# One sweep of a warp-and-blend kernel: the subtraction of the old feature on TensorE in every row, and a gate product over all 128 array rows

## The reference

```python
center = einsum('nchw,oc->nohw', feature, w_center)
step = relu(einsum('nchw,oc->nohw', feature, w_step))
prob = sigmoid(einsum('nchw,oc->nohw', feature, w_prob))
offset = center * step
th = minimum(round(gh + offset[0]), h - 1); tw = minimum(round(gw + offset[1]), w - 1)
tgt = mod(th * w + tw, h * w)
sample = grid.at[tgt].set(grid)            # a scatter: the last writer of a target wins
sampled = grid_sample_bilinear(feature, sample)
proped = sampled * prob + feature * (1 - prob)
return feature * prob + proped * (1 - prob)
```

## Time and profile before

| | us |
|---|---|
| median of 3 runs | 8082.5 (8072.88 to 8084.91) |
| the profiled execution, its own time | 8102.3 |
| its span | 8100.6 |
| TensorE busy | 5697.9 |
| VectorE busy | 5391.9 |
| GpSimd busy | 4030.2 |
| ScalarE busy | 3005.0 |
| mean granted clock of TensorE | 0.78 |

### The profile page before, as it was taken

One profiled execution on the slowest core, in us unless ns is written; L12 is line 12 of the kernel. 1 busy time (PEld: TensorE's weight loads), 2 busy tenths in 40 slices (PEclk: granted clock), 3 DMA queues, 4 the chain that ended last, 5 costly groups with the idle time before them and its releaser, 6 DMA issues. The chain is left out here.

```text
span 8100.6 us, 91641 instructions
## 1 busy us (share of the span) xinstructions
PE 5697.9 (70%) x26004; PEld 2956.5 (36%) x26004; DVE 5391.9 (67%) x12584; ACT 3005.0 (37%) x5830; POOL 4030.2 (50%) x8123
## 2 busy tenths in 40 slices
PE   5653645466756886689767676799677656878888
PEld 3432323233423443355443332354333222333333
DVE  6447774385754544866789735777889735777777
ACT  3432223122212332222112225666336545454545
POOL 6657453374434353634225336644335355666664
PEclk8876766688866886789877777899887777676777
DMA  7985569567556786666426776755235645666666
GB/s 278 354 306 194 175 210 276 170 235 240 187 163 204 282 291 217 223 206 211 155 91 233 223 261 212 216 160 167 91 112 173 166 143 177 209 214 214 213 215 193
DMA packets 543221, 1672.95 MB, mean 207 GB/s; under 512 B 125182, under 2 KB 180339, under 8 KB 501012
## 3 DMA queue, kind: packets, MB, share of 16 engines
q1 hardware_dynamic: 223708, 827.34, 33.3%
q10 hardware_dynamic: 254552, 763.42, 25.1%
q0 software_dynamic: 64480, 76.57, 5.1%
HBM read 949.39 MB, written 727.71 MB: 207 GB/s over the span
## 5 line engine op out<-in xcount | busy, mean ns | idle before, releaser
L1107 DVE TENSOR_TENSOR ps<-ps,arena 128x400 f32<-128x400 f32 x1600 | 929.1, 581 | 1853.5 <-PE ps L1286 657.3
L1416 ACT ACTIVATE arena<-ps 128x400 f32<-128x400 f32 x1600 | 800.8, 501 | 3155.7 <-PE ps L1270 1103.6
L1049 POOL TENSOR_TENSOR arena<-arena 128x32 f32<-128x32 f32 (+8 forms) x3013 | 941.9, 356 | 1910.6 <-PE ps L1312 1910.3
L1278 PE MATMUL ps<-arena,minus 128*128 128x400 f32 x2800 | 1625.5, 669 | 84.6 <-DVE arena L1109 84.2
L1326 PE MATMUL ps<-ident,arena 128*128 128x128 f32 x5000 | 916.5, 332 | 800.8 <-ACT arena L1390 469.3
L1295 PE MATMUL ps<-arena 128*64 128x400 f32 x3200 | 900.2, 646 | 602.4 <-ACT arena L1430 420.7
L1248 POOL DMA_INDIRECT arena<-table,gidx x800 | 871.5, 1089 | 843.7 <-PE ps L1295 552.8
L1390 ACT ACTIVATE arena<-ps 128x512 f32<-128x512 f32 (+1 forms) x1400 | 735.4, 551 | 1254.4 <-PE ps L1326 700.2
L1286 PEld LDWEIGHTS ps<-ident,arena 100*128 100x128 f32 x6400 | 833.5, 164 | 779.1 <-issue 642.3
L1326 PEld LDWEIGHTS ps<-ident,arena 128*128 128x128 f32 x5000 | 745.6, 204 | 988.4 <-ACT arena L1390 554.3
L1248 POOL DMA_INDIRECT arena<-table,arena x800 | 794.0, 992 | 528.8 <-issue 233.9
(11 more groups left out here) (212 smaller groups left out, 6216.8 us busy)
## 6 DMA issues: line engine op xcount, KB each, us to landing
arena<-x SPq DMA_DIRECT2D x200, 1600.0 KB
arena<-table SPq DMA_DIRECT2D x400, 800.0 KB
table<-arena ACTq DMA_DIRECT2D x400, 512.0 KB
y<-arena ACTq DMA_DIRECT2D x200, 800.0 KB
arena<-y SPq DMA_DIRECT2D x100, 1600.0 KB
out<-arena ACTq DMA_DIRECT2D x200, 800.0 KB
table<-arena ACTq DMA_DIRECT2D x200, 576.0 KB
conv<-arena ACTq DMA_DIRECT2D x800, 31.2 KB
```

The costliest lines, as they stand in the source:

```text
L1049: last = E.tensor_tensor(tmp[:, :, at:at + size], cols[:, :, y + to:end + to:step], cols[:, :, y:end:step], ALU.subtract)
L1107: V.tensor_tensor(d, d, g, ALU.mult).then_inc(s_mix, 1)
L1278: nc.tensor.matmul(ps[:, sums(r), 0:W], minus[:, :], tile(t)[:, r * W:(r + 1) * W], start=True, stop=False)
L1416: nc.scalar.activation(gate[r % 2], ps[:, 6 + r % GB, 0:W], ACT.Copy).then_inc(s_gcopy, 1)
```

## The change

In the last sweep the subtraction of the old feature is made by TensorE in every row: `lifted` and VectorE's L1104, with the semaphore between it and the multiplication, go. In all sweeps the gate product reads all 128 partitions of the gates' buffers (`gates_all`) and of `halves`, which grows from 24 to 128 partitions. What is not gate or weight in them is set to zero once: for two of the buffers and `halves` by VectorE at the start, for the third by GpSimd at the start of the fifth sweep, with a wait of SyncE before the first load into it. The loads write the same 24 partitions as before.

```diff
-        halves = sb("halves", [QUAD + 6 * HALF, HALF * 128], BF16)[QUAD:, :]
+        halves = sb("halves", [128, HALF * 128], BF16)
...
+        gates_all = [again(a, W, 128, BF16) for a in gates_at]
...
-                sp.wait_ge(s_init, 1)
+                sp.wait_ge(s_init, 2)
...
+                nc.vector.memset(halves[:, :], 0.0).then_inc(s_init, 1)
+                for a in range(2):
+                    nc.vector.memset(gates_all[a], 0.0)
...
-                nc.vector.tensor_copy(halves, halves32)
+                dve.wait_ge(s_init, 2)
+                nc.vector.tensor_copy(halves[QUAD:QUAD + 6 * HALF, :], halves32)
...
-            def lifted(r):
-
-
-                return listed and u_idx is None and r % 2 == 1
...
-                        if lifted(r):
-                            V.tensor_tensor(d, d, y, ALU.subtract).then_inc(s_less, 1)
-                            less[0] += 1
-                            dve.wait_ge(s_less, less[0])
                         V.tensor_tensor(d, d, g, ALU.mult).then_inc(s_mix, 1)
...
+                            if listed and j == RR - 1 and u_idx is not None:
+                                sp.wait_ge(s_blank, 1)
+                                alone(sp, "sp")
...
+                    if listed and u_idx is not None:
+                        nc.gpsimd.memset(gates_all[2], 0.0).then_inc(s_blank, 1)
...
-                        nc.tensor.matmul(ps[:, 6 + r % GB, 0:W], halves[:, m % HALF * 128:(m % HALF + 1) * 128], gates_in[j % RR],
+                        nc.tensor.matmul(ps[:, 6 + r % GB, 0:W], halves[:, m % HALF * 128:(m % HALF + 1) * 128], gates_all[j % RR],
                                          start=True, stop=True).then_inc(s_gate, 1)
...
-                        if not lifted(r):
-                            nc.tensor.matmul(ps[:, sums(r), 0:W], minus[:, :], tile(t)[:, r * W:(r + 1) * W], start=True, stop=False)
+                        nc.tensor.matmul(ps[:, sums(r), 0:W], minus[:, :], tile(t)[:, r * W:(r + 1) * W], start=True, stop=False)
...
-                                                    ident[0:STRIP, 0:STRIP], is_transpose=True, start=lifted(r) and q == 0, stop=not listed and q == STRIPS - 1)
+                                                    ident[0:STRIP, 0:STRIP], is_transpose=True, start=False, stop=not listed and q == STRIPS - 1)
```

More of the change, by code:

```diff
@@ L367, in _ @@
                     nc.vector.memset(w_conv[l][:, 10:], 0.0)
-                nc.vector.tensor_copy(halves, halves32)
+                dve.wait_ge(s_init, 2)
+                nc.vector.tensor_copy(halves[QUAD:QUAD + 6 * HALF, :], halves32)
                 nc.vector.tensor_copy(ident16[:, :], ident[:, :])
                 nc.vector.tensor_scalar(minus[:, :], ident[:, :], -1.0, None, ALU.mult).then_inc(s_init, 1)
-                dve.wait_ge(s_init, 2)
+                dve.wait_ge(s_init, 3)
         s_maps = sem("s_maps")
@@ L385, in build @@
         s_gatest = sem("s_gatest")
+        s_blank = sem("s_blank")
         s_path = sem("s_path")
@@ L390, in build @@
         tabled, rowed = [0], [0]
-        s_less, less = sem("s_less"), [0]
         s_fld = [sem(f"s_f_ld{a}") for a in range(4)]
```

## The result

The kernel takes 7890.06 us (median of 5 runs, 7851.52 to 7893.64) against 8072.88 us for the kernel before on the same chip (5 runs, 8067.68 to 8084.91): a ratio of 0.975, 95% interval 0.9719 to 0.9781. The profiled execution has a span of 7849.9 us; it is the fastest of its five, 39 us under their median, while the profiled execution before lies 29 us above this median of 8072.88.

The account below looks back on a forecast made before the run. TensorE was taken as the bound, often at half clock after waiting on ScalarE: 171 us off the last sweep plus 40 off the others takes 8102 to 7891, forecast as 7875 us since the profiled execution is 20 above the median; range 7760 to 8060.

Parts of the forecast that it names:

- The border of the gate product: TensorE, each row: each border of the 24-row product costs about 0.09 us; padding saves 36 us in the last sweep.
- The other sweeps: Mixing sweeps before the last: 30 us from 210 TensorE-bound rows plus 10 for the clock, 40 us less; bounds 0 and 150.
- The clock of the last sweep: TensorE, last sweep: share at half clock falls from 56% to 25%, so the granted clock rises from 0.72 to 0.87.
- The pause on ScalarE's L1430: TensorE's wait every four rows, last sweep: 3.5 us path fits in 3.6 us of rows, so most of 180.0 us goes.
- GpSimd's floor: Last sweep: two gathers a row, each 0.99 us plus 0.29 of issue, allow no less than 2.56 us a row.
- The landings: Last sweep: waits on landings of transfers, 7.4% of the chain, 97 us or 0.24 a row, do not go.
- transfers become the bound: Rival, last sweep: landings replace the pauses, 3.1 us a row, 70 us saved plus 20 elsewhere, about 7990 us; chance 0.18.
- gate product counts everywhere: Rival: clock rises in all four mixing sweeps, 150 us instead of 40, last sweep 2.65 us a row, 7680 us; chance 0.10.
- The exposed weight load: Rival: a 0.25 us load stands bare behind each gate product, last sweep only 31 us less, 8050 us; chance 0.03.
- The clock does not rise: Rival, last sweep: clock stays at 0.72, a row takes 3.6 us, kernel 130 us slower, 8210 us; chance 0.13.
- nothing: Rival: longer TensorE rows and fewer pauses cancel, 8080 us; chance 0.06.
- The clears: Clears on VectorE at the start and GpSimd before the fifth sweep: hidden, cost nothing; those on VectorE under 2 us if uncovered.

Follow-up runs that it names:

- 64-row: Kernel after the change, with the gate product over array rows 0 to 63 instead of 128: 8047.91 us, ratio 0.9904 to the kernel before.
- 72-row kernel: Kernel after the change, with the gate product over array rows 0 to 71 instead of 128: 7945.42 us, ratio 0.9763 to the kernel before.
- the move alone: Kernel after the change, but gate product on 24 rows again; only the last sweep's subtractions moved to TensorE: 8102.69 us, ratio 0.9958 to the kernel before.
- groups of eight: Kernel after the change, with GpSimd gathering in groups of eight rows instead of four in the last sweep: 8144.05 us, ratio 1.0024 to the kernel before.

## Why the prediction was right, and where its steps were not

The time was forecast at 7875 us in a range of 7760 to 8060, and is 7890. The total is right by luck: two steps miss in opposite directions.

**The border of the gate product** was priced at 0.09 us, and twice that where the product in front is a full one too. This term was mis-sized. The start of the subtraction after the gate product moved by 0.09 us, as forecast; but the subtraction is two products with a weight load each, and with the first load under the gate product what separates them shrinks as well, 0.11 us from its start to the transposes' (the earlier trace rows against the timeline after). A row in the two last sweeps thus saves 0.20 us; where a product over the full width of the array stands in front of the gate product, as transposes do in the two sweeps before, one more border of 0.09 us goes. The border in front of it after the 64-column one-hot products stayed, as forecast. The 64-row and 72-row kernels show that all of the row's saving is one step of shape.

**The other sweeps** were given 40 us, with 150 as the bound, because only 210 rows were taken to have TensorE as the limit. This step failed. 183 us are gone there in the profiled executions; over the ten profiles with at least 72 rows that share the code of these sweeps, the three windows sum to 5096 to 5168 us (mean 5137), against 5279 before and 5306 and 5261 with 24 and 64 rows, so the gain is 111 to 183 us. TensorE's saving of 149 us in the first of them became 65 us of time: only a part of it, but far more than 210 rows at 0.18 us could give. The last sentence of the prediction took a move of more than 100 us as a sign that "the gate product's width did more than its borders"; it came, and it came for the most part through the borders, not through the clock.

**The clock of the last sweep** was forecast at 0.87 and is 0.89. It does rise with the move alone (0.72 to 0.85). But the mix of products does not set it by itself, as the prediction's main choice had it: with the same mix it is 1.00 without the gathers and 0.81 with groups of eight. What it was to bring did not come: the move alone is worth 14 us. The last sweep gave 74 us of the 171 forecast, or 35 in the 72-row kernel.

**The pause on ScalarE's L1430** was to close, and most of its 180.0 us to go. This step failed: it is 197.1 us. The forecast row was 2.55 us of TensorE and 0.30 of waits, 2.85; the measured one is 2.11 / 0.89 = 2.37 and 0.74, 3.11. The comparison of 3.5 against 3.6 us was sound, as the run without gathers shows, but it started the 3.5 us at the recorded end of the one-hot products, and with gathers under way the multiplications of rows 3, 4, 7 and 0 start about 2 us later than that (medians of 1.8 to 2.1 us from row 40 on; before they were 1.1 to 1.5, with 0.6 for the subtraction in rows 3 and 7). It is mostly the counts of rows 3 and 7 that are late: there everything else that the multiplication waits for has long ended (by 1.9 and 1.3 us in the median), while in rows 4 and 0 it starts 0.1 us after the copy of the gate. GpSimd's floor, 2.56 us a row, was also short of what is behind it: after eight gathers of 1.25 us GpSimd waits 2.0 us (median) for a late count, so four rows cost 12.2 us, 3.05 each. That the count is held until GpSimd has finished is not shown. The forecast that GpSimd would be near 70% busy fails with it: 64%.

**The landings** were to stay at 7.4% of the chain, 97 us or 0.24 a row of the sum. The share stayed (7.4%), but the step is wrong: what stands there are releases that the profile cannot name, in front of VectorE's multiplication (102.5 us), ScalarE's copy of the gate and GpSimd's gathers (62.1 us), which wait for counts of other engines. They grow when bytes are taken out and are gone without the gathers. So this term of the sum is a part of the late counts and no price of transfers. The rival *transfers become the bound* named the last sweep's row (3.1 us) by the wrong mechanism: 30% fewer bytes change nothing, and only without gathers do landings of the table's rows become the wait. The rival *gate product counts everywhere* had the other sweeps' 150 us right, but not the clock as the main cause. *The exposed weight load* had it the wrong way round: the first load starts with the padded gate product, and it is behind the 24-row product that it had to wait. The Trainium skill, "TensorE: Matmul & The Clock Gate", The mechanism (in its Part 3), has a load overlap products in flight only where the row groups differ. The trace does not agree: here both use the full array and they overlap (7099.72 both), and the row got shorter by 0.20 us. *The clock does not rise* and *nothing* are ruled out by the time. (The first of them counts 1.94 us for a row of before; by the prediction's own terms, 2.31 and 1.53 in turn, it is 1.92, which changes nothing.)

**The clears** cost nothing that shows: the first gate copy stands at 1510 us after, 1504 before, and at 1491 to 1521 in the runs with the same clears.

What stays open is how GpSimd's gathers hold the other engines' progress. Ruled out are the two other waiters, the store, the gate's landing, the gathers' landing, bandwidth and one fixed pause to a group. Shorter stretches of gathers were not tried. Whether TensorE's products truly end late or only their counts are late, the trace does not tell, since the ends of products are modelled.

## What to carry to other kernels

A product over few array rows between full-array products can cost its neighbours as much as itself (0.20 us a row here, against the 0.18 after which it gives way): look at the start-to-start times on both sides, at the next product's own duration and at when its weight load begins, and fill the missing rows with zeros until the load begins early. A stage with a rising clock and falling busy time need not get faster; before pricing a stall by the recorded end of a product, compare it with when the waiting engine really started. A release that the profile cannot name is no landing until a run with fewer bytes has shown it. And where a total comes out right, check its parts by windows: here 171 + 40 was 35 to 74 and 111 to 183.

## What was not expected of the hardware

The shape of one bf16 product changes the one after next: with 24 or 64 array rows the following pair of f32 products takes 0.78 us to the next line, with 72 or 128 0.67, in addition to the 0.09 us at the border itself. With 72 or 128 the weights of that pair begin to load together with the bf16 product, with 24 or 64 only 0.27 us later.

While GpSimd issues indirect transfers back to back, the waiters on TensorE's products start late against the products' recorded ends, and together: 4.4 us after them, and 1.6 us after the eighth gather, in the piece of the kernel after; 11.4 us after them in the piece with sixteen gathers. Taking the gathers out of one sweep shortens it from 1244 to 893 us, although GpSimd's own 1.25 us a gather, 2.5 a row, would leave room for a sweep of 1000.
